# Attention and feed-forward block on one core: five slices of the middle tile's values in the even gap and three in the odd one, where four stood in each

## What is computed

```python
q_weights = exp(sum((q - centers)**2) * inv_var)        # same for k
logits = einsum('bihs,bjhs,hs->bijh', q_weights, k_weights, amplitudes)
attention = softmax(logits / temp, axis=2)
out = einsum('bijh,bjhd->bihd', attention, v) @ out_w.T
x = x + out
...
r = sigmoid(xr @ W_r.T);  k = square(relu(xk @ W_k.T))
x = x + r * (k @ W_v.T)
```

## Time and profile before

| | |
|---|---|
| median of 3 runs | 2138.8 us (2138.59 to 2140.33) |
| the profiled execution | 2140.03 us |
| its span | 2138.2 us |
| TensorE busy | 2108.5 us, 99% |
| ScalarE busy | 2003.9 us, 94% |
| VectorE busy | 822.9 us, 38% |
| granted TensorE clock, mean | 0.998 of full speed |

### The profile page before, as it was taken

How to read it: one execution, slowest core, us unless ns; L and a number is a source line. 1 busy time by engine, 2 the same in 40 slices (tenths; PEclk the granted TensorE clock), 3 DMA queues, 4 the chain that set the end, 5 groups by cost and what they waited for, 6 DMA issues and landing times.

```text
span 2138.2 us, 52139 instructions
## 1 busy us (share of the span) xinstructions
PE 2108.5 (99%) x22756; PEld 947.4 (44%) x22756; DVE 822.9 (38%) x1886; ACT 2003.9 (94%) x2184; POOL 398.1 (19%) x502
## 2 busy tenths in 40 slices
PE   7999999999999999999999999999999999999999
PEld 4444444444444444444444444444444444443445
DVE  6123433332436252524425225262244334514236
ACT  4999999999999999999999999999999999999995
POOL 0243342424242020220402202204000000000000
PEclk9999999999999999999999999999999999999999
DMA  6534444436533315124241421612422141221111
GB/s 196 140 94 124 120 130 127 122 90 169 126 113 98 73 61 156 34 89 118 73 136 44 125 83 49 164 36 76 110 58 55 40 90 41 44 63 34 34 41 45
DMA packets 176489, 193.59 MB, mean 91 GB/s; under 512 B 88656, under 2 KB 108496, under 8 KB 176240
## 3 DMA queue, kind: packets, MB, share of 16 engines
q1 hardware_dynamic: 166720, 174.69, 29.4%
q0 software_dynamic: 7424, 15.22, 2.9%
q10 hardware_dynamic: 2096, 0.14, 0.1%
HBM read 98.90 MB, written 75.81 MB: 82 GB/s over the span
## 4 chain that ended last, share of the span: by engine, by line
PE 79%; ACT 17%; DVE 3%; issue 1%; DMA 0%; DVEq 0%; ACTq 0%
PE ps_pv L1000 35%; PE ps_scores L981 24%; PE ps_step L1028 16%; ACT probs L1325 15%; PE ps_step L1049 1%; DVE h_t L1675 1%; ACT weight L1385 1%; PE ps_scores L1018 0%; PE ps_scores L1013 0%; PE ps_scores L1176 0%; DVE mixed_r L1660 0%; PE ps_scores L1022 0%; DMA x_prep<-x 0%; ACT gate L1382 0%; DVE gate_in L1628 0%
## 5 line engine op out<-in xcount | busy, mean ns | idle before, releaser
L1325 ACT ACTIVATE probs<-ps_scores 128x1024 f32<-128x1024 f32 x2048 | 1938.1, 1037 | 82.2 <-PE ps_scores L981 54.1
L1000 PE MATMUL ps_pv<-probs,vals 128*32 128x512 f32 (+5 forms) x9760 | 1071.8, 531 | 1.1 <-DVE o_raw L1690 1.1
L981 PE MATMUL ps_scores<-q_aug,k_aug 49*128 49x512 f32 x4096 | 707.3, 439 | 11.8 <-ACT probs L1325 7.8
L981 PEld LDWEIGHTS ps_scores<-q_aug,k_aug 49*128 49x128 f32 x4096 | 331.6, 184 | 635.5 <-ACT probs L1325 591.6
L1000 PEld LDWEIGHTS ps_pv<-probs,vals 128*32 128x32 f32 x9760 | 335.8, 139 | 208.7 <-issue 121.0
L1443 POOL DMA_DIRECT2D packed<-qk x232 | 116.9, 509 | 830.3 <-DVE qk L1617 802.7
L1448 POOL TENSOR_TENSOR packed<-qk 32x512 f32<-32x512 f32 x232 | 246.9, 1064 | 17.5
L1453 POOL TENSOR_TENSOR k_act<-k_act 128x512 f32<-128x512 f32 x28 | 29.1, 1040 | 825.0 <-DVE k_act L1620 825.0
L1690 DVE COPY o_raw<-ps_pv 128x512 f32<-128x512 f32 x63 | 43.6, 691 | 266.2 <-PE ps_pv L1000 266.0
L1617 DVE COPY qk<-ps_step 128x512 f32<-128x512 f32 x58 | 40.0, 690 | 216.6 <-PE ps_step L1028 216.4
L1620 DVE TENSOR_SCALAR k_act<-ps_step 128x512 f32<-128x512 f32 x29 | 20.0, 691 | 236.9 <-PE ps_step L1028 236.9
(11 more groups left out here) (217 smaller groups left out, 1101.7 us busy)
## 6 DMA issues: line engine op xcount, KB each, us to landing
k_aug<-k_parts SPq DMA_DIRECT2D x128, 192.0 KB, 4.6
q_aug<-q_parts SPq DMA_DIRECT2D x128, 192.0 KB
k_parts<-parts SPq DMA_DIRECT2D x31, 512.0 KB, 3.2
q_parts<-parts SPq DMA_DIRECT2D x31, 512.0 KB, 3.2
packed<-qk POOLq DMA_DIRECT2D x232, 64.0 KB, 2.2
x_ffn<-x SPq DMA_DIRECT2D x18, 512.0 KB, 5.3
vals<-v_kept SPq DMA_DIRECT2D x64, 128.0 KB, 5.2
k_parts<-parts SPq DMA_DIRECT2D x31, 256.0 KB, 3.4
```

What stands on the lines that cost most here:

```text
L981: mm = pe.matmul(ps_scores[:, g % RING, e, :], k_aug[rows, s % 2, pair, kt * P:(kt + 1) * P], q_aug[rows, u % 2, pair, :], start=True, sto ...
L1000: mm = pe.matmul(ps_pv[32 * c:32 * c + 32, at], vals[:, s % 2, kt, :, c], probs[:, tick % PROB_SLOTS, c, at], start=(kt == 0), stop=(kt == ...
L1325: act.activation(probs[:, tick % PROB_SLOTS, 2 * pair:2 * pair + 2, :], ps_scores[:, g % RING, :, :], ACT.Exp).then_inc(probs_ready, 1)
```

## The change

Where the loads of both gaps of a pair are equal and the middle tile is split, one slice more stands in the even gap: five and three in place of four and four.

```diff
@@ -515,7 +515,8 @@
     kt = (3 * m - 1) % KT
     if kt in (0, KT - 1):
         return SLICES if kt else 0
-    early = round(SLICES / 2 + SLICES / 4 * (load(2 * m + 1) - load(2 * m)))
+    alike = load(2 * m + 1) == load(2 * m)
+    early = round(SLICES / 2 + SLICES / 4 * (load(2 * m + 1) - load(2 * m))) + int(alike)
     return 0 if early < 2 else SLICES if early > SLICES - 2 else early
```

## The result

The changed kernel took 2142.39 us in the median of 20 runs (2140.05 to 2145.82), the kernel before 2138.84 in 20 runs beside it (2137.85 to 2141.60). The ratio is 1.0013, with a 95% interval of 1.0007 to 1.0019, so +1.5 to +4.1 us and +2.8 in the middle. This is the ratio of the means; the medians lie 3.55 apart. The forecast was 2141.4 and +2.6, in a range of 2137.4 to 2143.0. The change costs time, by less than the 0.2% that the forecast set as its bound.

What follows compares the result with a forecast made beforehand. TensorE and ScalarE hold each other, neither alone bounding the kernel. 22 pairs at 0.107 less 0.10 gave +2.25, nine without work +0.4: +2.65 us on median 2138.8, so 2141.4 us, range 2137.4 to 2143.0.

Steps and rivals of the forecast that it cites:

- The bound: Main loop: a fill begins at the later of gap start + 0.89 and the previous gap's third exponential's end + 0.47.
- A slice is 0.107: Fill of each touched gap: one slice lengthens the even fill and shortens the odd one by 0.107 us.
- Two pieces: Pairs with two pieces of work per gap: next even gap starts 0.11 sooner, its fill later; pair costs 0.107 us.
- Three pieces: Pairs with three pieces of work per gap: next even gap starts as before, its fill 0.107 us later.
- The 8 with a ScalarE extra: Pairs with a tanh or weight exponential behind the even gap's exponentials: waiting swallows the shift, cost 0.
- The 9 without work: Pairs without side work, both engines at their limit: together 0 to 0.96 us, taken as +0.4.
- The sum: All 42 touched pairs together: +2.65 us, giving 2141.4 us from the median; bounds 4.5 either way.
- The rule on weight loads: Third score pair: the skill has loads pulled ahead, but the row showed the load behind the wait; forecast followed the row.
- A wait costs only itself: First rival: fill follows the exponential's end by 0.37, so three-piece pairs cost 0.01; +1.5 us, 2140.3, chance 0.07.
- Columns only: Rival: a pair's columns are unchanged and TensorE is 99% busy, so +0, 2138.8 us; chance 0.16.
- Evening out: Rival: in two-piece pairs exponentials reach the next pair 0.11 sooner; ten pairs give -1.1, 2137.7 us; chance 0.12.
- Narrow sets: Rival: late sets of 192 columns held by their weight loads; at 0.03 per set 2143.9 us; chance 0.05.

Runs made afterwards that it cites:

- the run with the group moved: Third score group put behind the fill's first values after each of 25 pairs, against the kernel before; four and four 2144.48 us, with five and three 2146.81.
- the first and third run: Against the kernel before, only the 25 pairs with equal side work and no even-gap ScalarE extra: five and three 2140.88 us (1.0013), six and two 2144.47 (1.0024).
- the chosen table: Early slices set by the prediction's rule in 37 pairs, 16 of them from eight to six, against the kernel before; 2136.83 us, ratio 0.9992.
- the second table: Early slices set from a table in only 19 pairs, against the kernel before; 2136.68 us, ratio 0.9992.

## Why the prediction was right

**The bound.** That the two engines hold each other through the ring of three was the step everything hung on, and the runs agree with it: the odd fill starts at 3.87 or 3.88 after the pair with three, four and five early slices, though its gap starts at 2.68, 2.79 and 2.89. The control is the run with the group moved: with nothing to wait for, the same shift wins 0.11 in ten of the 11 two-piece pairs.

**A slice is 0.107.** The rows agree: the even fill ends 0.10 later and the odd one lasts 0.12 less, and one slice and two cost 2.44 and 4.98 in the stretch.

**Two pieces: 0.107 each.** Read at the fill of the next even gap, 10 of 11 pairs cost 0.09 to 0.14 in the change, the eleventh 0.02.

**Three pieces: 0.107 each.** 13 of 14 cost 0.10 to 0.13 at the same place. The one I had at -0.10 measured -0.09, and the two-piece pair that I had at 0 cost 0.02. The three-piece pair that I had at 0 (pair 191) stands at 0.11 there, but at the start of pair 193 only 0.01 of it is left, so in the sum it is near the 0.

**The 8 with a ScalarE extra: 0.** Measured, in sum, -0.02. In the pair around 261 the next even gap starts sooner, and the third weight load follows 6.79 after the pair, as before (6.80):

```profile
259.48 0.30 PEld L982 LDWEIGHTS ps_scores<-q_aug,k_aug 49*128 49x128 f32 x4 [0.81 <-ACT probs L1326]
...
266.27 0.19 PEld L982 LDWEIGHTS ps_scores<-q_aug,k_aug 49*128 49x128 f32 x2 [0.73 <-ACT probs L1326]
```

**The 9 without work: +0.4, between 0 and 0.96.** This term was mis-sized: eight of them cost 0.02 in sum, the lower bound (the ninth is the last pair of the program and has no scores behind it). I had put ScalarE's cover at about half; that the exponentials run back to back there and that TensorE waits 0.4 in each gap fits a cover that takes the shift whole.

**The sum.** 2.65 forecast, 2.40 in the trace's stretch, 2.8 (1.5 to 4.1) over the runs. The 25 pairs with work gave 2.44 as the only ones changed, where 2.25 was forecast, and those without work about 0 where 0.4 was, so two small misses partly cancel. The median came 1.0 above the forecast, and some of that may be the beginning, which no term covers: in the trace it made 1.2 of the 3.6. The range was wide and held the case of no change as well, so the number alone proves little; the single pairs and the moved group do.

**The rule on weight loads.** The row decided, rightly. In the Trainium skill, TensorE: Matmul & The Clock Gate (Step-by-step: what each phase is for), TensorE pulls weight loads ahead of matmuls in flight. With the load pulled ahead, the three-piece pairs would have cost about 0.01 by the first rival's sum. They cost 0.11, and where the third score pair waits, its load starts 0.05 us after the exponential's end (154.34 against 154.29 before, 158.47 against 158.42 after). The section says nothing of a load that stands behind a wait of its own, so these rows mark a limit of the rule and don't contradict it.

**The rivals.** A wait costs only itself: the fill behind the three-piece pair would have come at 6.90 or 6.91, and it came at 7.01. Columns only: the first and third run exclude it (+2.4 and +5.0). Evening out: the pair does end sooner (5.63, 5.55), and the time is still lost. Narrow sets: the odd fills get shorter by the whole slice, down to 128 columns.

## What to carry to other kernels

Where two engines pass slots of a ring back and forth, the end of a stage is the wrong place to read a shift: it ended 0.11 sooner and the work behind the next wait began 0.11 later. Write down for each stage the two times of which the later one starts it, and carry both through two stages; here that gave nearly every pair with side work to 0.03 us, and missed where a cover of ScalarE had to be guessed. Moving work helps only where the time that it moves is the one that binds, and time won on one engine can be held next by a chain that was just in time (near the end of the run with 37 pairs it was VectorE's).

## What was not expected of the hardware

The start of the main loop is not alike from run to run. In the window 50 to 54 the granted clock of TensorE was at its lower level (1.2 GHz) in the kernel before and at its upper one (2.4 GHz) in the kernel with the chosen table, and the code there is the same in both. Columns: busy time of PE, PEld, DVE, ACT, POOL, then the granted clock, DMA share and GB/s.

```profile
50.00:54.00 4.00, 4.00 (x16) 1.18 (x16) 0.74 (x5) 3.26 (x4) 0.00 (x0) 0.50 1.04 310
```

```profile
50.00:54.00 4.00, 3.31 (x26) 1.16 (x30) 0.40 (x3) 4.00 (x6) 0.00 (x0) 1.00 1.03 309
```

Just before, from 46 to 50, TensorE had been busy 2.4 of 4 us in both. Of the second table's 11 runs, the six with a mean clock of 0.999 or 1.000 took 2135.9 to 2136.7, and the five with 0.998 took 2138.1 to 2138.7: two microseconds, nearly as much as the change itself. The 15 runs of the kernel before beside it are less clean: nine with 1.000 took 2138.1 to 2139.4, and six with 0.999 or 0.998 took 2138.7 to 2142.0. From the first exponential to the 13th the traces took 12.0 to 16.6 us. That the clock alone makes the two microseconds isn't shown: the wait for `k_aug` in the kernel after lies in the same place.
